# Maxima of the first quad inside the projection phase, halves, quarters and pairs of key tiles in a gated attention kernel

## The reference, cut to what matters

```python
x = L0_attn_x                              # 2 x 2048 x 512, float32
xn = layernorm(x)                          # no gain, no bias
q, k, v = xn @ Wq, xn @ Wk, xn @ Wv        # 16 heads of 32
scores = einsum('bthd,bshd->bhts', q, k) * tril(ones)   # masked scores are 0, not -inf
attn = softmax(scores / 2048 ** 0.5)
s = (attn @ v) @ Wo
g = silu(layernorm(xn, gamma, beta) @ ternary(weight).T + bias)
out = x + s * g
```

## Time and profile before

| | |
|---|---|
| Median of 3 runs | 1652.95 us (1650.23 to 1656.3) |
| Profiled execution | 1653.39 us |
| Its span | 1651.6 us |
| Mean granted TensorE clock | 0.954 |
| Busy: PE, DVE, POOL, ACT | 1540.7, 1049.1, 885.5, 770.2 us |

### The profile page before, as it was taken

One profiled execution on the slowest core, in us unless ns is written; L12 is line 12 of the kernel. 1 busy time (PEld: TensorE's weight loads), 2 busy tenths in 40 slices (PEclk: granted clock), 3 DMA queues, 4 the chain that ended last, 5 costly groups with the idle time before them and its releaser, 6 DMA issues.

```text
span 1651.6 us, 24364 instructions
## 1 busy us (share of the span) xinstructions
PE 1540.7 (93%) x8554; PEld 913.3 (55%) x8554; DVE 1049.1 (64%) x2357; ACT 770.2 (47%) x1614; POOL 885.5 (54%) x725
## 2 busy tenths in 40 slices
PE   6999999993999999999999999999999999799977
PEld 5788888882545445544544454444544454333755
DVE  7555445532977776776777677776777677700657
ACT  4333333320026655655665565665665565467210
POOL 4000000003027777778777776876777777768541
PEclk9999999996559999999999999999999999999988
DMA  6656556557901035045035105403603500131998
GB/s 207 194 179 194 175 181 202 179 178 181 226 27 40 21 84 142 21 90 142 22 85 113 61 28 118 114 21 84 154 21 84 142 21 14 56 113 33 291 338 300
DMA packets 109977, 201.34 MB, mean 122 GB/s; under 512 B 14368, under 2 KB 32288, under 8 KB 108832
## 3 DMA queue, kind: packets, MB, share of 16 engines
q1 hardware_dynamic: 98768, 177.79, 39.6%
q10 hardware_dynamic: 11088, 22.02, 4.1%
HBM read 123.22 MB, written 76.28 MB: 121 GB/s over the span
## 4 chain that ended last, share of the span: by engine, by line
PE 75%; DVE 10%; DMA 7%; ACT 3%; POOL 2%; issue 2%; SPq 1%; ACTq 0%; POOLq 0%; DVEq 0%
PE psP L1180 19%; PE psS L1272 16%; PE psO L1295 16%; PE psM L1247 13%; PE psL L1301 6%; DMA gr<-gate 4%; DVE mx L1053 3%; DVE psM L1050 2%; PE psL L1310 2%; ACT Pb L871 2%; PE psT L1140 2%; POOL acc L750 1%; PE psM L1272 1%; DMA Ks<-k_lo 1%; DMA Qs<-mrow 1%
## 5 line engine op out<-in xcount | busy, mean ns | idle before, releaser
L750 POOL TENSOR_TENSOR acc<-acc,Pb 128x1024 f32<-128x1024 f32 (+2 forms) x308 | 597.8, 1970 | 131.5 <-PE psO L1295 100.4
L871 ACT ACTIVATE Pb<-psS 128x512 f32<-128x512 f32 (+3 forms) x1101 | 503.0, 531 | 346.0 <-PE psS L1272 330.0
L1053 DVE TENSOR_REDUCE mx<-psM 128x1 f32<-128x512 f32 x722 | 458.8, 684 | 170.8 <-PE psM L1247 170.0
L1272 PE MATMUL psS<-Qs,Ks 97*128 97x512 f32 (+1 forms) x1223 | 468.7, 403 | 14.6 <-ACT Pb L871 7.4
L1247 PE MATMUL psM<-Ks,Qs 96*128 96x512 f32 (+3 forms) x1218 | 439.2, 395 | 34.7 <-DMA Ks<-k_lo 24.8
L1272 PEld LDWEIGHTS psS<-Qs,Ks 97*128 97x128 f32 x1223 | 227.4, 191 | 281.3 <-ACT Pb L871 115.7
L1050 DVE CUSTOM_DVE_ANT_0 psM<-psM,negm 128x128 f32<-128x128 f32 (+3 forms) x496 | 229.6, 517 | 116.4 <-PE psM L1247 115.9
L1247 PEld LDWEIGHTS psM<-Ks,Qs 96*128 96x128 f32 x1218 | 231.9, 197 | 100.4 <-DVE mx L1053 25.8
L1295 PE MATMUL psO<-Pb,Vs 128*32 128x512 f32 (+3 forms) x2304 | 272.0, 539 | 11.9 <-POOL Pb L733 11.9
L733 POOL TENSOR_SCALAR_AFFINE_SELECT Pb<-Pb 128x256 f32<-128x256 f32 x240 | 94.1, 405 | 119.5 <-ACT Pb L871 117.2
L686 POOL TENSOR_TENSOR rstd<-ve,mhalf 128x4 f32<-128x4 f32 x8 | 8.1, 1010 | 242.0 <-DVE ve L941 241.9
(11 more groups left out here) (107 smaller groups left out, 1650.7 us busy)
## 6 DMA issues: line engine op xcount, KB each, us to landing
Qs<-q_hi SPq DMA_DIRECT2D x32, 512.0 KB, 12.9
Ks<-k_hi SPq DMA_DIRECT2D x32, 512.0 KB, 11.1
xt<-in_L_attn_x SPq DMA_DIRECT2D x8, 1024.0 KB, 7.1
q_hi<-st_hi SPq DMA_DIRECT2D x32, 256.0 KB, 3.6
q_lo<-st_lo SPq DMA_DIRECT2D x32, 256.0 KB, 3.4
gate<-gs SPq DMA_DIRECT2D x32, 256.0 KB, 2.2
k_hi<-st_hi SPq DMA_DIRECT2D x32, 256.0 KB, 2.6
k_lo<-st_lo SPq DMA_DIRECT2D x32, 256.0 KB, 2.8
```

The costliest lines, as they stand in the source:

```text
L750: g.tensor_tensor(to[:, :, o:], to[:, :, o:], Pb[s % RING][:, heads, o:], ALU.add).then_inc(sum_done, 1)
L871: a.activation(weights(s, h)[:, o:], score_bank(s * HQ + h, last)[:, o:], ACT.Exp, scale=SCALE).then_inc(exp_done, 1)
L1053: ins = v.tensor_reduce(flat[:, heads, slots], bank[:, 0:ns * w].rearrange("p (a b c) -> p a b c", a=nh, c=w), AX.X, ALU.max)
L1272: t.matmul(score_bank(n, last)[:, o:], Ks[par][0:MROW + 1, h, j * P:(j + 1) * P], Qs[par][0:MROW + 1, h, c * CW + o:(c + 1) * CW], start=T ...
```

## The change

Five things change together.

1. **Early maxima.** The 38 banks of quad 0's lower half and their two turns run inside the projection phase, in chunks 3 to 7: one entry behind each of the last two query products, the four gate products and the first two key products. They use two banks, those of `psT[2]` and `psT[3]`. SP loads quad 0's lower halves at the end of chunk 2's key stores, and in chunk 7, behind the last key store, the row maxima, the first chunk's sums, the values, and quad 0's upper halves. The stage in which 117 banks run alone is gone.
2. **Shares.** Quad 0's other 102 banks run beside its first 19 steps (43 in the first eight, 59 in the next eleven). Every quad now has its last 65 banks beside its own first 19 steps and the next quad's first 75 beside the other 21. In the last quad the six score banks serve only chunk c = 3.
3. **Halves.** `Qs` and `Ks` are four buffers of 1024 tokens a quad, laid out so that early ones lie beside what the projection phase uses. The row of ones comes by a DMA.
4. **Quarters.** Row maxima are made for each 512 rows; one turn carries both kinds of maxima, where two turns carried 1024 rows. Narrow banks hold one query tile for several heads.
5. **Pairs.** PE runs the scores and maxima of two steps in a row, then the values of two steps. Within a slot the maxima bank comes ahead of the score tile, except for the last head of an odd step.

The diff, cut to its core (planner, then SP's order in the projection phase, then PE's):

```diff
-    for r in range(1, CT):
-        w = r * P
-        for half in range(2):
...
+    for i in range(NT):
+        w = (i + 1) % CT * P
+        if w:
+            slot = i * MXC + (i + 1) // CT
+            heads = max(1, CW // w)
+            for h in range(0, HQ, heads):
...
-OWN_STEPS = 7
+OWN_STEPS = 19
+FIRST_STEPS = 8
...
 def step_time(s):
-    return width(s) + P
+    c, j = STEPS[s]
+    return width(s) + P - (2 * P if c and j == 0 else 0)
+
+def maxima_first(s, h):
+    return s % 2 == 0 or h < HQ - 1
...
 def max_entries():
...
+    early = max_order([(0, k) for k in range(NLOW)])
+    pieces = [(0, 0, FIRST_STEPS, [(0, k) for k in range(NLOW, ENDS[2])]), (0, FIRST_STEPS, OWN_STEPS, [(0, k) for k in range(ENDS[2], NMB)])]
+    for qn in range(NQUAD):
+        if qn:
+            pieces.append((qn, 0, OWN_STEPS, [(qn, k) for k in range(UPFRONT, NMB)]))
+        pieces.append((qn, OWN_STEPS, NSTEP, [(qn + 1, k) for k in range(UPFRONT) if qn + 1 < NQUAD]))
...
 def max_bank(n):
-    return n % (2 * NBS) if n < NUP else n % NBS
+    return 1 + n % 2 if n < NEARLY else n % NBS
...
+EARLY_CHUNKS = range(NCH - 1, 2 * NCH)
+EARLY_SLOTS = 2 * CT
+EARLY_SHARE = -(-NEARLY // len(EARLY_CHUNKS))
...
+def early_slot(product, m):
+    return {"queries": m - 2, "gate": 2 + m, "keys": 6 + m if m < 2 else -1}[product]
...
-        WIDE = STEPS.index((2, 0)) * HQ
+        WIDE = STEPS.index((3, 0)) * HQ
...
+                if n == EARLY_CHUNKS[0] - 1:
+                    for k in range(4):
+                        sp.wait_ge(st_out[k], START + 2 * 2 * 32)
+                    sp.wait_ge(whi_done, 3)
+                    sp.wait_ge(wlo_done, 3)
+                    load_half(0, 0, 0)
+                    load_ones(0, 0)
+                if n == NCHUNK - 3:
+                    store_maxima(0, 0)
+                if n == NCHUNK - 1:
+                    store_maxima(0, 1)
+                    sp.wait_ge(P_full, START + n * NPU + AT_GATE + CT)
+                    load_chunk(0, 0)
+                    load_values(0, 0)
+                    load_half(0, 0, 1)
+                    load_ones(0, 1)
+                    load_chunk(0, 1)
...
+            def early(n, slot):
+                entries = early_share(n, slot)
+                if entries:
+                    pe.wait_ge(const_c, FOR_MAXIMA)
+                    pe.wait_ge(cs_done, START + n * NQ)
+                max_scores(entries)
...
-            phase_a_over(pe)
-            pe.wait_ge(const_c, FOR_MAXIMA)
...
-            max_scores(range(NUP))
-            pe.wait_ge(const_c, FOR_SCORES)
+            pe.wait_ge(vs_done, NCHUNK * CT)
...
                     for h in range(HQ):
+                        beside = max_share(qn, slots, h) if slots is not None else []
+                        if slots is None or maxima_first(slots, h):
+                            max_scores(beside)
                         if ahead:
                             scores(*ahead, s, h, not more)
-                        if slots is not None:
-                            max_scores(max_share(qn, slots, h))
+                        if slots is not None and not maxima_first(slots, h):
+                            max_scores(beside)
...
-                for s, (c, j) in enumerate(STEPS):
+                if qn == 0:
+                    pe.wait_ge(cs_done, START + NCHUNK * NQ)
...
+                for gr, (c, j) in enumerate(GROUPS):
+                    s = 2 * gr
+                    ahead(s)
+                    ahead(s + 1)
                     values(s)
                     if j == 0 and (c > 0 or follows):
                         row_sums(*((qn, c - 1, not more) if c else (qn - 1, NCH - 1, False)))
+                    values(s + 1)
```

More of the change, by code:

```diff
@@ L57, in max_banks @@
                 banks.append(([(h, i, f * CW, CW)], slice(h, h + 1), slice(i * MXC + f, i * MXC + f + 1)))
-    for r in range(1, CT):
-        w = r * P
-        for half in range(2):
[L61 to L69, removed]
+    for i in range(NT):
[4 more added lines that the diff above has]
+            for h in range(0, HQ, heads):
+                banks.append(([(h + x, i, (i + 1) // CT * CW, w) for x in range(heads)], slice(h, h + heads), slice(slot, slot + 1)))
     return banks
@@ L75, in diagonal, with quarter_of @@
     return k0 + w == (tile + 1) * P
-def half_of(bank):
-    return bank[0][0][1] // HALF
-MAXB = sorted(max_banks(), key=half_of)
+def quarter_of(bank):
+    return bank[0][0][1] // CT
+MAXB = sorted(max_banks(), key=quarter_of)
 NMB = len(MAXB)
-NLOW = sum(half_of(bank) == 0 for bank in MAXB)
+ENDS = [sum(quarter_of(bank) <= q for bank in MAXB) for q in range(NCH)]
+NLOW = ENDS[1]
 def width(s):
@@ L134, in max_order @@
         if due and len(order) >= due[0][0]:
[L135 to L152, removed]
@@ L155 @@
-SLOTS = max_slots()
-def max_entries():
[L160 to L170, removed]
+            order.append(("turn", *due.pop(0)[1:]))
+    return order + [("turn", *d[1:]) for d in due]
+def max_entries():
+    early = max_order([(0, k) for k in range(NLOW)])
[4 more added lines that the diff above has]
+        pieces.append((qn, OWN_STEPS, NSTEP, [(qn + 1, k) for k in range(UPFRONT) if qn + 1 < NQUAD]))
+    order = max_order([bank for piece in pieces for bank in piece[3]])
+    shares, start = {}, 0
+    for z, (qn, first, end, banks) in enumerate(pieces):
+        upto = order.index(("bank", *banks[-1])) + 1 if banks else len(order)
+        if z == len(pieces) - 1:
+            first, end = first, first + 2
+        steps = [(s, h) for s in range(first, end) for h in range(HQ)]
+        whole, past, k = sum(step_time(s) for s, _ in steps), 0, start
+        for s, h in steps:
+            past += step_time(s)
+            to = start + (upto - start) * past // whole
+            shares[qn, s, h] = range(len(early) + k, len(early) + to)
+            k = to
+        start = upto
+    return early + order, len(early), shares
@@ L264, in build @@
         pc = ExitStack()
[L265 to L269, removed]
         Pb = [sbuf(pc, f"Pb{i}", [P, HQ, CW], F32) for i in range(RING)]
@@ L351, in build @@
         const_c = sem("const_c")
-        FOR_MAXIMA, FOR_SCORES = 4, 6
+        FOR_MAXIMA = 4
+        ones_in = [[sem(f"ones_in{i}{half}") for half in range(2)] for i in range(2)]
         kq_low = [sem(f"kq_low{i}") for i in range(2)]
@@ L499, in _, with load_half, heads @@
             load_x(1)
+            def load_half(qn, par, half):
+                cols = slice(half * T // 2, (half + 1) * T // 2)
+                def heads(a):
+                    return a[bass.ds(qn * P, P), cols].rearrange("(h d) t -> d h t", d=DH)
+                into = (kq_low, kq_high)[half][par]
+                for g, (qa, ka) in enumerate(((q_hi, k_hi), (q_lo, k_hi), (q_hi, k_lo))):
+                    rows = slice(g * DH, (g + 1) * DH)
+                    sp.dma_start(Qs[par][half][rows].bitcast(F32), heads(qa)).then_inc(into, 16)
+                    sp.dma_start(Ks[par][half][rows].bitcast(F32), heads(ka)).then_inc(into, 16)
@@ L532, in _ @@
             phase_a_over(sp)
[L534 to L544, removed]
@@ L1068, in reciprocals @@
+            chunks(chunk)
             def reciprocals(b):
@@ L1070, in reciprocals @@
                 v.reciprocal(lr[:], lr[:]).then_inc(lrec_done, 1)
-            maxima(range(NUP))
             def numerators(qn, c):
```

339 lines of the change are left out of this document (182 added, 157 removed).

## The result

The changed kernel takes 1641.23 us (1638.31 to 1648.25, 9 runs), the kernel before 1653.49 (9 runs): ratio 0.9937, 95% interval 0.992 to 0.9955. That is 12 us faster where 38 were forecast. One execution of a later run, single_scores_first, took 2048.16 us at a mean granted clock of 0.653 and is left out; all others stand within 1% of their like. The profiled execution's span fell from 1651.6 to 1638.8.

What follows compares the result with a forecast made beforehand. PE was taken to bound the kernel (93% busy), except a stage before quad 0 where DVE reduces maxima banks alone. +10 - 64 + 9 + 8 - 1 = -38 from 1653.4 gave 1615 us; own range 1592 to 1640.

Steps and rivals of the forecast that it cites:

- part 4: Six middle quads: pairs and front tiles give 133.6 us a quad against 132.0, +9 us in all.
- Part 1: First phase: 38 of quad 0's banks added, 8.5 us, plus 1.5 for a held-up transfer, +10 us.
- Part 2: Between first phase and quad 0: PE stands 14 us for the upper halves, plus 3 for low clock afterwards.
- Part 3: Quad 0 with 102 own banks and 75 of quad 1: 169 us with the pause, against 233, -64.
- The recurrence: Middle quads and quad 0: a bank's weights load when the reduce three banks earlier is done; its matmul starts 0.235 us later.
- DVE's burst: Full pair: eight banks every 0.47 us onto three buffers, DVE needs 0.593 each; run 4.27 us instead of 3.89.
- run of pair 14: Middle quads: a run of scores with narrow bank pieces, claimed to take 6.2 us instead of 4.1.
- Part 5: Last quad: own banks go from 23 to 65, +8 us; score banks serving only c=3 save 1.
- The rival of the full switch saving: If DVE's lag is caught up, six middle quads give -36 us instead of +9; 1565 in all, chance 0.12.
- The rival through ScalarE: Pairs: eight exps from three score banks make each run 0.8 us longer, +112; 1727 in all, chance 0.08.
- The load gap: Before quad 0: upper halves queue behind chunk 7's stores, landing 30 us after PE's end; 1631 in all, chance 0.12.
- first-phase rival: First phase: each of 38 banks makes PE wait 1.1 us for its reduce, 42 in all; 1650, chance 0.08.

Runs made afterwards that it cites:

- single_scores_first: The changed kernel with PE's order by single steps and the score tile ahead of the maxima bank in every slot: 1614.62 us, ratio 0.9766.

## Why the prediction was wrong

Right in direction, wrong in size, by one term, part 4: +29 for +9. Two steps of it failed, and both had been put at nothing.

- **Part 1, first phase**: +13.6 for +10. The banks are right, 8.3 us with the buffers at 1024 bytes for 8.5 forecast; the 1.5 for transfers was nothing, and 5.3 came from the buffers' place, which was not seen: the text took the layout to cost nothing by leaving it out.
- **Part 2, the pause**: 15.5 for 14, PE's wait ended by the upper halves as named. Clock 0.62 in that window.
- **Part 3, quad 0**: 152.7 for 155.
- **Part 4, the clock**: the text has PE in the middle quads "at full clock" and no term for it. Its own rows show 0.95 for steps 8 to 19 of quad 3; the kernel before has 10.2 us at clock 0.50 in the six quads, and with the change it is 27.3. The recurrence is made of prices at full clock and gave 133.6 us; at full clock the changed quad takes 134.6, as it ran 136.9. So 2.3 of the missing 3.3 us a quad, 14 of the 20 us, are the clock. What makes it fall more often with pairs was not tried.
- **Part 4, POOL's sum behind ScalarE**: "exps keep 0.515 to my 0.53 per score, inside DVE's delay" counts ScalarE's own pace and not what it waits for. The exponentials of a pair's second step wait for POOL's sum, and so the last score of the run stands: a full pair takes 7.3 us for 7.0, with DVE's passes cut too, and 6.93 with POOL's halved. At full clock POOL's halving is worth 2.2 us a quad. "The saving is eaten where tiles are full" is so, but DVE's burst, rightly sized at 4.27 (4.22 measured), eats only a part; elsewhere the recurrence took too much (run of pair 14: 6.2, measured 5.5), which hides half of POOL's part. The run free of waits comes to 3.76 + 0.17 = 3.93 by the text's own prices, not 3.89, and to 4.1 measured with both engines out.
- **Part 5, last quad**: +9.5 for +7. The 6.3 us it starts from hold some 1.6 of clock (an estimate: 3.4 us of that window were at 0.50, and such a stretch cost the pair at 773.24 1.6 us).
- **The rival of the full switch saving** is refuted for this kernel. The price of a visit was read well (0.30 us), but with DVE and POOL out only 1.7 of 6 us a quad come back, 3.5 at full clock.
- **The rival through ScalarE** was right that ScalarE lengthens the run, by 0.34 for its 0.8; but the cause is POOL's sum and not ScalarE's pace, and only five of a quad's twenty pairs change by more than 0.2 us when POOL's sums are halved.
- **The load gap and the first-phase rival** did not come: 15.5 us for 30, and 8.3 us of banks for 42.

The Trainium skill's TensorEngine Tiling (Array Packing), section Key Properties, says that a change of tiling mode drains the engine. The rows show it as 0.09 + 0.11 + 0.10 us a visit; the runs show that avoiding it did not pay here. Its warning on emptying PSUM, in the section Performance Considerations, was weighed at 0.38 a run; the run came out 0.7 longer than 3.9, of which 0.3 stays when POOL's sums are halved.

## What to carry to other kernels

Where PE waits for an engine, ask what that engine waits for: here a matmul stood for ScalarE, and ScalarE for a sum on POOL. Where a wait is put to an engine that had long been done, look for another on which the same instruction waits. An engine at 70% of a quad can still bound a burst: compare, for each stretch that an order makes, how many buffers stand ready and how long their reader takes for one. Doubling a block to halve a switch also doubles the burst. Read the granted clock beside every difference, before it is shared out among waits. A change of order should be timed apart from the change of work it comes with: here one gained some 37 us and the other gave 25 back.

## What the runs showed of the hardware that was not expected

Matmuls of 128x512 that read float32 operands from buffers displaced by 1028 or 1088 bytes start every 0.232 to 0.234 us, from buffers at multiples of 1024 bytes every 0.227, with weights and streams alike in all else. In the quads the step from a bank's matmul to a score's has a median of 0.234 to 0.238 in all of these kernels, and does not follow the placement in the same way.

The granted clock fell to 0.50 inside stretches where PE was busy 97% of the time (797.34 of 821.43 us), for 27.3 us with pairs and for 3.4 with the same work by single steps.
